# Three more row places in the adapted-attention layers, the output bias as its own step, retention's last transpositions among its gate projections, and the last pool sums on TensorE

## The chip, the cores and the metric

The kernel runs on the 8 cores of one Trainium2 chip. Each core computes one sequence of the batch by itself; the cores do not talk to each other. The metric is the device time of one launch in microseconds (us), taken on the slowest core. Five engines of a core run their own instruction queues: PE (TensorE, matrix products), DVE (VectorE), ACT (ScalarE), POOL (GpSimd) and SP, which here only starts transfers (DMA). They wait for each other by semaphores.

## The reference, cut to what matters

One sequence has 2048 tokens of width 1024. Four layers follow each other, each with a residual sum and a layer norm without weights ahead of it:

```
x = x + attn_a(layernorm(x))     # causal softmax attention, 16 heads of 64, projections q, k, v, o
x = x + ffn(layernorm(x))        # full attention, its q, k, v, o weights adapted (below), biases on each
x = x + attn_b(layernorm(x))     # retention: v is scanned along the tokens, y = q*state, layer norm of y,
                                 # times silu(x @ Wg.T), then @ Wo.T
x = x + ffn(layernorm(x))        # the same as the second, with the same weights
```

The adapted weights of `ffn` come from a gate: the mean of the layer's normed input over all tokens, two small products, the best 2 of 8 experts, and for each of q, k, v, o a low-rank product that is added to the main weight. So nothing of `ffn` can be projected until every token tile of the layer before has been normed and summed.

## The kernel before, in words

The program names the layers `a`, `f1`, `b`, `f2`. A token tile is 128 tokens; there are 16, numbered `t` or `tt` from 0. The residual rows live in memory (tensor `Xs`, at the start `xin`, at the end `y`); on the core there is only their normed and transposed form, in the arenas `XA` and `XB`. A layer reads its input from one arena (`ARENA[L][0]`) and keeps its attention output (`ctx`) in the other.

**What happens to a token tile at the end of a layer.** Two output projections `O` of 8 matmuls each (128x512, line 992) make the halves of the tile. DVE adds each to the tile's residual row in place (line 1266). The row was loaded (`xl`, line 1586) into one of three row places, number `t % 3`. In the layers `f1` and `f2` POOL has before that added the output bias `OB` to the whole row (line 1534, called `ob` here); before the change this add is part of the step `xl`, so it stands in POOL's queue where the load stands in SP's. After the second half the row is stored (`xs`, line 1591) and, but for `f2`, normed: statistics on DVE (`ln1`, lines 1337 and 1340), the reciprocal root on POOL (`rs`, lines 1442 and 1445), the norm itself on DVE (`ln2`, line 1349), which reads a 128x1024 row of f32 and writes bf16. PE transposes the normed tile (`T`, line 996), DVE or ACT copies it to the next layer's arena (lines 1272 and 1147). In `a` and `b`, POOL also adds the normed tile to a running sum (`pr`, line 1454), which the gate of the next layer reads. Then the next row is loaded into the place, tile `t + 3`: SP waits until the store of tile `t` has landed and `ln2` of it has run.

**What sets the order.** A planner (`Plan`, `build_plan`) writes one list of steps; each engine's part of the program walks this list and takes what is its own. So each queue holds its steps in the list's order, and a step that waits holds up everything behind it on its engine. The steps `rs` and `ln2` are put 1 and 2 groups of PE work behind the tile's last projection (`norm`).

**Where the tiles are done.** In `a`, `f1` and `f2` the projections of tiles 0 to 7 lie in the attention of the second half of the tokens (`second_half`), where ACT's exponentials run nearly without a gap. Tiles 8 to 15 come after it, alone (`tail`, `o_dense`). I call this stretch the tail of the layer. It starts when the attention of the last head pair has been divided by its sums: DVE takes reciprocals (line 1309), copies them apart in 8 copies (line 1316) and multiplies (line 1326); PE has by then done 7 of 8 matmuls of the first four projections. In `b` the tokens go in 4 chunks of 512 (`c`). A chunk projects v and q for 8 slices (`bv`, `bq`, line 1000), then sums over the slices on PE (`bs`, line 1005), then projects the gate for 8 slices (`bg`). DVE and POOL norm the slices (`bz`), ACT applies scale and silu, and DVE multiplies (`bap`, line 1380). The output projections of the 4 tiles of the chunk before lie among the v and q projections; tiles 12 to 15 form the tail of `b`. Their `T` of the last two tiles of a chunk stand right ahead of `bs`.

**The gate** (lines 1094 to 1105): after the tail of `a` or `b`, PE sums the running sum over the partitions by 8 f32 matmuls of one column (line 1094). It waits for the last `pr` and for all evictions.

Of the kernel before, what the change touches and what calls it, by code (L numbers as in the profile page):

```python
# [13 lines left out]
T = 2048  # L14
# [8 lines left out]
FFN = ("f1", "f2")  # L23

# [30 lines left out]
class Plan:  # L55
# [38 lines left out]
    def special(self, a):  # L94
        if a[0] == "rs":
            self.count("rs", ("rs",) + a[1:])
        elif a[0] == "ln2":
            self.count("ln2", ("ln2",) + a[1:])
        self.step(*a)
        if a[0] == "ln2":  # L100
            L, t = a[1:]
            if L in ("a", "b"):
                self.count("pr", ("pr", L, t))
                self.step("pr", L, t)
            if t + 3 < NT:
                self.xl(L, t + 3)
# [33 lines left out]
    def after(self, grp):  # L140
# [11 lines left out]
        elif k == "O" and a[1] == 1:  # L152
            t = a[0]
            self.step("xs", L, t)
            if L != "f2":
                self.norm(L, t)
            elif t + 3 < NT:
                self.xl(L, t + 3)
# [40 lines left out]
def build_plan():  # L199
    P = Plan()  # L200

    def o_items(L, tiles, by="v"):
# [252 lines left out]
    def second_half(L, k_ch):  # L455
# [4 lines left out]
        if L == "a":  # L460
            out.insert(at_[NP - 2], ("f_pre", "f1"))
# [120 lines left out]
    def b_layer():  # L582
# [8 lines left out]
        for c in range(4):  # L591

            o = {}
            if c >= 1:
                its = o_items("b", list(range(4 * c - 4, 4 * c)))
                n_o = [i for i, g in enumerate(its) if isinstance(g, Grp) and g.kind == "O" and g.args[1] == 0]
                o = {3: its[:n_o[1]], 4: its[n_o[1]:n_o[2]], 6: its[n_o[2]:n_o[3]], 7: its[n_o[3]:]}
# [12 lines left out]
            for d in range(ND):  # L610
# [54 lines left out]
def build_program():  # L665
# [147 lines left out]
    dXL = [sem(f"d_xl{i}") for i in range(3)]  # L813
    dXS = [sem(f"d_xs{i}") for i in range(3)]
# [21 lines left out]
    n = {"xl": [0] * 3, "xs": [0] * 3}  # L836
    for st in P.steps:
        if st[0] == "xl":
            s_ = st[2] % 3
            n["xl"][s_] += 16  # L840
            dv[("xl", st[1], st[2])] = n["xl"][s_]
        elif st[0] == "xs":
            s_ = st[2] % 3
# [45 lines left out]
    with nc.Block("main") as blk:  # L889
# [3 lines left out]
        def _(t_):  # L893
# [113 lines left out]
            for st in P.steps:  # L1007
# [75 lines left out]
                elif st[0] == "gate":  # L1083
# [104 lines left out]
        def _(v_):  # L1188
# [15 lines left out]
            for st in P.steps:  # L1204
                if st[0] == "att_on":
                    v.wait_ge(dCO, NCO)
                if st[0] == "fe" and st[1].by == "v":
# [52 lines left out]
                    elif k == "O":  # L1260
# [3 lines left out]
                        v.wait_ge(dXL[tt % 3], dv[("xl", L, tt)])  # L1264
# [39 lines left out]
                elif st[0] == "gn":  # L1304
# [14 lines left out]
                    else:  # L1319
                        cl = i - 8  # L1320
                        v.wait_ge(vSF, gn_at[5 + 2 * cl])
                        if g.L in FFN and g.h == 0 and g.p == 0:

                            for tt in (13, 14, 15):
                                v.wait_ge(dXS[tt % 3], dv[("xs", "a" if g.L == "f1" else "b", tt)])
# [3 lines left out]
                elif st[0] == "ln1":  # L1329
                    _, L, tt = st  # L1330
                    if L == "x":
                        v.wait_ge(dXL[tt % 3], dv[("xl", L, tt)])
# [98 lines left out]
        def _(g_):  # L1431
# [5 lines left out]
            for st in P.steps:  # L1437
# [128 lines left out]
        def _(p_):  # L1566
            p = Eng(p_)
            for st in P.steps:
                if st[0] == "xl":
# [4 lines left out]
                    else:  # L1574
# [4 lines left out]
                        if tt >= 3:  # L1579
                            p.wait_ge(dXS[tt % 3], dv[("xs", L, tt - 3)])  # L1580
                            if L != "f2":
                                p.wait_ge(vXN, at[("ln2", L, tt - 3)])
                        if L != "a":
                            before = {"f1": "a", "b": "f1", "f2": "b"}[L]
                            p.wait_ge(dXS[tt % 3], dv[("xs", before, tt)])
                    p_.dma_start(xo(L, tt), dr[SRC[L]][tt * 128:(tt + 1) * 128, :]
                                 ).then_inc(dXL[tt % 3], 16)
                elif st[0] == "xs":
# [3 lines left out]
                                 ).then_inc(dXS[tt % 3], 16)  # L1592
# [33 lines left out]
            for i in range(3):  # L1626
# [57 lines left out]
```

## Time and profile before

| | us |
|---|---|
| median of the three runs shown | 2783.66 |
| lowest and highest of them | 2586.55, 2851.24 |
| the profiled execution | 2594.22 |
| its longest core (5), first to last instruction | 2592.5 |
| its shortest core (1) | 2567.9 |

On core 5 PE is busy for 85% of the span, ACT for 58%, DVE for 51% and POOL for 24%. The profile was taken of one execution; all rows below are of its core 5, and all times in them count from the core's first instruction.

### The profile page before, as it was taken

Reading aid. Unit: us, or ns where it says so; the run is one execution under the profiler, and the core shown is the slowest. Engines: PE = TensorE matmul, PEld = TensorE weight load, DVE = VectorE, ACT = ScalarE, POOL = GpSimd, SP = SyncE. Lnnn points to the kernel's source line nnn. Section 1 sums busy time; section 2 is a strip of 40 time slices with the busy share of each in tenths; the row PEclk is TensorE's granted clock in tenths of the full one; section 3 lists DMA queues with packets and bytes.
Section 4 is the critical chain, followed back from the end, with each engine's and each line's share of the span. In section 5 each row is a group of like instructions: output and inputs, shape, how many; then the busy total and the mean of one; then the engine's idle time right before and its main releaser. Section 6 shows DMA issues by size and latency. Waiting matters only on the chain.

```text
span 2592.5 us, 39690 instructions; the slowest of 8 cores (2567.9 to 2592.5 us)
## 1 busy us (share of the span) xinstructions
PE 2201.5 (85%) x13480; PEld 766.5 (30%) x13480; DVE 1317.0 (51%) x2018; ACT 1498.3 (58%) x1494; POOL 635.0 (24%) x762
## 2 busy tenths in 40 slices
PE   4888799998699989879899599996989989788886
PEld 2322222223342222222222244443422222222222
DVE  4367635656453444434554567775445454433443
ACT  1234377773007777879999032221057777899991
POOL 4244333434111111112212323333021211021112
PEclk9989899999699999999999899997999999999998
DMA  8111322224400000012211531135200000021003
GB/s 173 25 25 25 62 46 65 66 74 129 148 9 24 25 26 25 17 49 58 58 42 50 130 73 66 65 114 154 74 25 26 25 25 17 17 74 33 33 33 122
DMA packets 49570, 151.10 MB, mean 58 GB/s; under 512 B 6624, under 2 KB 8800, under 8 KB 49120
## 3 DMA queue, kind: packets, MB, share of 16 engines
q1 hardware_dynamic: 33984, 124.80, 14.8%
q0 software_dynamic: 13376, 23.07, 6.1%
q8 instruction: 115, 1.88, 0.3%
q10 hardware_dynamic: 2016, 0.70, 0.1%
q14 instruction: 79, 0.65, 0.1%
HBM read 138.06 MB, written 33.55 MB: 66 GB/s over the span
## 4 chain that ended last, share of the span: by engine, by line
PE 59%; ACT 12%; DVE 12%; issue 8%; DMA 5%; POOL 3%; ACTq 0%; DVEq 0%; POOLq 0%; SPq 0%
ACT MISC L1135 11%; PE psd L1045 10%; PE psx L1064 8%; PE psx L974 6%; PE psx L970 6%; PE psx L1079 6%; PE psx L992 4%; PE psd L965 3%; PE psx L1000 3%; PE psx L965 3%; PE psd L1000 3%; PE psx L978 1%; DVE MISC L1316 1%; DMA XB<-Xs 1%; DVE MISC L1309 1%
## 5 line engine op out<-in xcount | busy, mean ns | idle before, releaser
L1135 ACT ACTIVATE MISC<-psd,NEGC 128x1024 bf16<-128x1024 f32 (+3 forms) x1344 | 1389.0, 1083 | 659.8 <-PE psd L1047 644.0
L1045 PE MATMUL psd<-MISC,KT 64*128 64x512 bf16 (+3 forms) x1344 | 510.2, 382 | 96.5 <-ACT MISC L1135 88.7
L1047 PE MATMUL psd<-MISC,KT 64*128 64x512 bf16 (+3 forms) x1344 | 514.8, 385 | 0.0
L1064 PE MATMUL psx<-MISC,VT 128*64 128x512 bf16 (+3 forms) x1344 | 424.1, 391 | 19.2 <-POOL MISC L1528 7.4
L1066 PE MATMUL psx<-MISC,VT 128*64 128x512 bf16 (+3 forms) x1344 | 425.9, 392 | 0.0
L1045 PEld LDWEIGHTS psd<-MISC,KT 64*128 64x128 bf16 x1344 | 124.4, 93 | 610.7 <-issue 603.5
L1521 POOL TENSOR_TENSOR MISC<-KT 128x512 bf16<-128x512 bf16 x96 | 108.3, 1128 | 565.8 <-DVE KT L1223 507.8
L1316 DVE COPY MISC<-MISC 32x512 f32<-32x512 f32 x384 | 218.6, 569 | 9.1
L1079 PE MATMUL psx<-MISC,ONESs 128*32 128x512 bf16 (+3 forms) x2688 | 218.9, 388 | 0.0
L1521 POOL TENSOR_TENSOR MISC<-MISC 128x512 bf16<-128x512 bf16 x96 | 106.8, 1113 | 339.2 <-DVE MISC L1230 282.4
L1309 DVE RECIPROCAL MISC<-MISC 128x128 f32<-128x128 f32 x192 | 170.0, 922 | 4.6
L1064 PEld LDWEIGHTS psx<-MISC,VT 128*64 128x64 bf16 x1344 | 97.9, 108 | 199.1 <-issue 198.1
L1534 POOL TENSOR_TENSOR XB<-XB,MISC 128x1024 f32<-128x1024 f32 x32 | 75.3, 2359 | 271.0 <-DMA XB<-Xs 271.0
L974 PE MATMUL psx<-XB,MISC 128*128 128x512 bf16 x504 | 128.9, 388 | 12.9 <-DVE MISC L1230 8.8
L1230 DVE TENSOR_SCALAR MISC<-psx,CST 128x512 bf16<-128x512 f32 x63 | 46.6, 739 | 163.3 <-PE psx L974 163.3
L1528 POOL TENSOR_TENSOR MISC<-MISC,TRIs 128x256 bf16<-128x256 bf16 x128 | 86.4, 676 | 159.3 <-ACT MISC L1135 157.6
L1047 PEld LDWEIGHTS psd<-MISC,KT 64*128 64x128 bf16 x1344 | 124.5, 93 | 0.0
L1223 DVE TENSOR_SCALAR KT<-psx,CST 128x512 bf16<-128x512 f32 x58 | 43.5, 751 | 158.6 <-PE psx L970 158.6
L970 PE MATMUL psx<-XB,MISC 128*128 128x512 bf16 x464 | 123.1, 394 | 0.0
L1066 PEld LDWEIGHTS psx<-MISC,VT 128*64 128x64 bf16 x1344 | 97.9, 108 | 0.0
L1301 DVE COPY MISC<-psx 128x512 f32<-128x512 f32 x48 | 33.2, 691 | 125.3 <-PE psx L1079 124.7
L1266 DVE TENSOR_TENSOR XB<-psx,XB 128x512 f32<-128x512 f32 x45 | 30.6, 682 | 130.2 <-PE psx L992 109.1
(187 smaller groups left out, 2707.6 us busy)
## 6 DMA issues: line engine op xcount, KB each, us to landing
XB<-Xs SPq DMA_DIRECT2D x40, 512.0 KB, 4.1
MISC<-fWq SPq DMA_DIRECT2D x32, 512.0 KB, 3.5
Xs<-XA SPq DMA_DIRECT2D x24, 512.0 KB, 3.0
Xs<-XB SPq DMA_DIRECT2D x24, 512.0 KB, 3.0
XB<-xin SPq DMA_DIRECT2D x16, 512.0 KB, 6.3
XA<-xin SPq DMA_DIRECT2D x16, 512.0 KB, 5.1
MISC<-fWk SPq DMA_DIRECT2D x16, 512.0 KB, 3.6
y<-XB SPq DMA_DIRECT2D x16, 512.0 KB, 3.0
```

Source lines behind the costliest of these rows:

```text
L965: return mm(o, xt(L, i, m * 128, 128), W1[:, i * 1024 + j * 512:i * 1024 + (j + 1) * 512], start=st, stop=sp)
L970: return mm(o, w[:, i * 128:(i + 1) * 128], xt(L, i, ch * CH, CH), start=st, stop=sp)
L974: return mm(o, w[:, i * 128:(i + 1) * 128], xt(L, i, h * 1024 + cl * CH, CH), start=st, stop=sp)
L1045: mm(pd[:, s:CH], ks[0:64, :], q[0:64, cl * CH + s:(cl + 1) * CH], start=True, stop=True, tile_position=(0, 0))
L1047: mm(pd[:, CH + s:2 * CH], ks[64:128, :], q[64:128, cl * CH + s:(cl + 1) * CH], start=True, stop=True, tile_position=(64, 0)).then_inc(sSC, 1)
L1064: mm(PVB[cl][0:64, s:CH], va[:, 0:64], r[:, s:CH], start=(c.tk == 0), stop=lastk, tile_position=(0, 0))
L1066: ins = mm(PVB[cl][64:128, s:CH], va[:, 64:128], r[:, CH + s:2 * CH], start=(c.tk == 0), stop=lastk, tile_position=(0, 64))
L1079: ins = mm(DENB[q0:q0 + 32, s:CH], ONES[:, 0:32], r[:, hd * CH + s:(hd + 1) * CH], start=(c.tk == 0), stop=lastk, tile_position=(0, q0))
L1135: s_.activation(r, pd, AF.Exp, bias=NEGC[:, col:col + 1], scale=sc).then_inc(aEX, 1)
L1309: chain(v_.reciprocal(d, d))
L1316: ins = v_.tensor_copy(RB[cl][32 * q:32 * q + 32, :], DN[q0:q0 + 32, :])
L1521: g_.tensor_mul(SQ[:, o:o + CH], src, src).then_inc(gSQ, 1)
```

## The change

- `slot` and `follower`: in `f1` and `f2`, tiles 11, 12 and 13 get row places of their own (3 to 5), in the second half of the input arena, which is free once the last q is projected. Their loads (`xl`) stand in the list ahead of the projections of tile 6, in the second half's attention. Tile `t` up to 7 is followed in its place by `t + 3`; tiles 8 and 9 by 14 and 15.
- The bias add is a step `ob` of its own. It stands where the projections of the tile before it begin.
- In `b`, the transpositions of the last two tiles of a chunk stand behind the gate projections of slices 1 and 3 and are copied by ACT instead of DVE. Tile 11 is projected in the tail instead of chunk 3.
- The running sum on POOL stops after 14 tiles. The gate's sum over the partitions adds the last two tiles from their normed rows: 16 bf16 matmuls of one column more.

```diff
+def slot(L, t):
+    return t % 3 + 3 if L in FFN and 11 <= t <= 13 else t % 3
+
+def follower(L, t):
+    if L not in FFN:
+        return t + 3
+    return t + 3 if t <= 7 else t + 6
...
-            if L in ("a", "b"):
+            if L in ("a", "b") and t < NT - 2:
                 self.count("pr", ("pr", L, t))
                 self.step("pr", L, t)
-            if t + 3 < NT:
-                self.xl(L, t + 3)
+            self.load_next(L, t)
...
             self.begin(grp)
+            if grp.kind == "O" and grp.args[1] == 0:
+                self.ob(grp.L, grp.args[0] + 1)
...
     def xl(self, L, t):
-        if L in FFN:
+        self.step("xl", L, t)
+
+    def ob(self, L, t):
+
+        if L in FFN and t < NT:
             self.count("ob", ("ob", L, t))
-        self.step("xl", L, t)
+            self.step("ob", L, t)
+
+    def load_next(self, L, t):
+
+        n = follower(L, t)
+        if n < NT and slot(L, n) == slot(L, t):
+            self.xl(L, n)
...
-                out += [("xl", L, x) for x in range(3)]
+                out += [("xl", L, x) for x in range(3)] + [("ob", L, 0)]
...
-        if L == "a":
-            out.insert(at_[NP - 2], ("f_pre", "f1"))
+
+        out[at_[NP - 2]:at_[NP - 2]] = [("f_pre", "f1")] if L == "a" else [("xl", L, t) for t in (11, 12, 13)]
...
-            o = {}
+            o, late = {}, []
             if c >= 1:
-                its = o_items("b", list(range(4 * c - 4, 4 * c)))
+
+                its = o_items("b", list(range(4 * c - 4, 4 * c - c // 3)))
                 n_o = [i for i, g in enumerate(its) if isinstance(g, Grp) and g.kind == "O" and g.args[1] == 0]
-                o = {3: its[:n_o[1]], 4: its[n_o[1]:n_o[2]], 6: its[n_o[2]:n_o[3]], 7: its[n_o[3]:]}
+                o = {3: its[:n_o[1]], 4: its[n_o[1]:n_o[2]], 6: its[n_o[2]:-2]}
+                if c < 3:
+                    o.update({6: its[n_o[2]:n_o[3]], 7: its[n_o[3]:-2]})
+                late = [Grp("T", "b", g.args, ND, 0.35, "a") for g in its[-2:]]
...
                 if d >= 2:
                     bap(c, d - 2)
+                if d % 2 and late:
+                    P.dense([late.pop(0)])
...
     def b_tail():
-        o_dense("b", list(range(12, NT)))
+        o_dense("b", list(range(11, NT)))
...
     def xo(L, t):
         a, base = scratch(L, t)
+        if slot(L, t) >= 3:
+            base += 8192
         base += (t % 3) * 2048
...
-                    t.wait_ge(gPR, at[("pr", src, NT - 1)])
+                    t.wait_ge(gPR, at[("pr", src, NT - 3)])
+                    t.wait_ge(vXN, at[("ln2", src, NT - 1)])
                     for dt in range(ND):
-                        ins = mm(BK[4][:, 16 + dt:17 + dt], ACC[src][:, dt * 128:(dt + 1) * 128], ONESF[:],
-                                 start=True, stop=True)
+                        o = BK[4][:, 16 + dt:17 + dt]
+                        mm(o, ACC[src][:, dt * 128:(dt + 1) * 128], ONESF[:], start=True, stop=False)
+                        mm(o, xn(src, NT - 2)[:, dt * 128:(dt + 1) * 128], ONES[:, 0:1],
+                           start=False, stop=False)
+                        ins = mm(o, xn(src, NT - 1)[:, dt * 128:(dt + 1) * 128], ONES[:, 0:1],
+                                 start=False, stop=True)
...
-                elif st[0] == "xl" and st[1] in FFN:
+                elif st[0] == "ob":
                     _, L, tt = st
                     g.wait_ge(dCO, NCO)
-                    g.wait_ge(dXL[tt % 3], dv[("xl", L, tt)])
+                    g.wait_ge(dXL[slot(L, tt)], dv[("xl", L, tt)])
                     g_.tensor_add(xo(L, tt), xo(L, tt), OB).then_inc(gOB, 1)
...
-                        if tt >= 3:
-                            p.wait_ge(dXS[tt % 3], dv[("xs", L, tt - 3)])
-                            if L != "f2":
-                                p.wait_ge(vXN, at[("ln2", L, tt - 3)])
+                        for t0 in range(NT):
+                            if follower(L, t0) == tt and slot(L, t0) == slot(L, tt):
+
+                                p.wait_ge(dXS[slot(L, t0)], dv[("xs", L, t0)])
+                                if L != "f2":
+                                    p.wait_ge(vXN, at[("ln2", L, t0)])
+                        if slot(L, tt) >= 3:
+                            p.wait_ge(sFL, at[("f", "Q", L, 1, NP - 1, 1)])
```

The order that comes out of it, at two places. In both, a name says what is written, then what is read; the line numbers of the changed kernel are other ones for the same steps.

First POOL, from the last attention of `f1` into its tail. L1534 (before) and L1573 (changed) are `ob`, L1442 and L1445 (L1481 and L1484) are `rs`. Before:

```order
L1561 DMA VT<-bWg 128x1024 x8
L1442 TENSOR_SCALAR RSD0<-MV0 128x1
L1445 TENSOR_TENSOR RSD0<-RSD0,PWR 128x1
L1534 TENSOR_TENSOR XB<-XB,MISC 128x1024
L1442 TENSOR_SCALAR RSD1<-MV1 128x1
L1445 TENSOR_TENSOR RSD1<-RSD1,PWR 128x1
L1534 TENSOR_TENSOR XB<-XB,MISC 128x1024
```

Changed:

```order
L1600 DMA VT<-bWg 128x1024 x8
L1573 TENSOR_TENSOR XB<-XB,MISC 128x1024 x2
L1481 TENSOR_SCALAR RSD0<-MV0 128x1
L1484 TENSOR_TENSOR RSD0<-RSD0,PWR 128x1
L1481 TENSOR_SCALAR RSD1<-MV1 128x1
L1484 TENSOR_TENSOR RSD1<-RSD1,PWR 128x1
L1573 TENSOR_TENSOR XB<-XB,MISC 128x1024
L1481 TENSOR_SCALAR RSD0<-MV0 128x1
L1484 TENSOR_TENSOR RSD0<-RSD0,PWR 128x1
L1573 TENSOR_TENSOR XB<-XB,MISC 128x1024
```

The adds of tiles 9 and 10 now stand ahead of the tail's first `rs`, and those of 11 to 15 each right behind an `rs`. Before, each stood behind an `rs` too, but was the add of a row that had just been asked for.

Second PE, in `b`, at the end of chunk 1's v and q projections (L1000 or L1034 with `KT`). L992 or L1026 is `O`, L996 or L1030 `T`, L1005 or L1039 `bs`, L1000 or L1034 with `VT` the gate projection. Before:

```order
L992 MATMUL psd1<-W1,XB 128x512 x8
L996 MATMUL psd1<-IDENTBs,XB 128x128 x8
L996 MATMUL psx0<-IDENTBs,XB 128x128 x8
L1005 MATMUL psx1<-MISC,ONESs 128x512 x8
L1005 MATMUL psx2<-MISC,ONESs 128x512 x8
L1000 MATMUL psx3<-XA,VT 128x512 x8
L1000 MATMUL psd0<-XA,VT 128x512 x16
```

Changed:

```order
L1026 MATMUL psd1<-W1,XB 128x512 x8
L1039 MATMUL psd1<-MISC,ONESs 128x512 x8
L1039 MATMUL psx0<-MISC,ONESs 128x512 x8
L1034 MATMUL psx1<-XA,VT 128x512 x8
L1034 MATMUL psx2<-XA,VT 128x512 x8
L1030 MATMUL psx3<-IDENTBs,XB 128x128 x8
L1034 MATMUL psd0<-XA,VT 128x512 x16
L1030 MATMUL psd1<-IDENTBs,XB 128x128 x8
```

The two `T` moved from ahead of `bs` to behind the second and the fourth gate projection; chunks 2 and 3 have the same.

## Rows read from the trace of the kernel before

**Rows 1.** One line of the cores: span and mean granted TensorE clock (1 is full speed).
```profile
core 5: 2592.5 us, clock 0.944
```

**Rows 2.** The page's chain that ended last, shares of the span by engine.
```profile
PE 59%; ACT 12%; DVE 12%; issue 8%; DMA 5%; POOL 3%; ACTq 0%; DVEq 0%; POOLq 0%; SPq 0%
```

**Rows 3.** Timeline, f1's tail: an ln2 while POOL is free.
```profile
1440.94 0.81 DVE L1349 TENSOR_SCALAR XB<-XB,MV,RSD 128x1024 bf16<-128x1024 f32 x1 [0.49 <-POOL RSD L1445]
```

**Rows 4.** Timeline, f1's tail: start us, us, engine line [idle before <-releaser]; PE, POOL.
```profile
1441.90 0.61 PE L996 MATMUL psx<-IDENTBs,XB 128*128 128x128 bf16 x8 [1.62 <-DVE XB L1349]
...
1450.90 2.34 POOL L1534 TENSOR_TENSOR XB<-XB,MISC 128x1024 f32<-128x1024 f32 x1 [10.07 <-DMA XB<-Xs]
...
1498.27 1.01 PE L996 MATMUL psd<-IDENTBs,XB 128*128 128x128 bf16 x8 [3.71 <-DVE XB L1349]
```

**Rows 5.** Timeline, a's tail: PE's transpositions of two tiles in a row.
```profile
634.66 0.61 PE L996 MATMUL psd<-IDENTBs,XA 128*128 128x128 bf16 x8 [0.32 <-DVE XA L1349]
...
639.04 0.61 PE L996 MATMUL psd<-IDENTBs,XA 128*128 128x128 bf16 x8 [0.33 <-DVE XA L1349]
```

**Rows 6.** Timeline near 53 us: POOL's rs, its next step, DVE's ln2.
```profile
52.99 0.57 POOL L1445 TENSOR_TENSOR RSD<-RSD,PWR 128x1 f32<-128x1 f32 x1
53.52 1.04 POOL L1521 TENSOR_TENSOR MISC<-MISC 128x512 bf16<-128x512 bf16 x1
...
53.66 1.45 DVE L1349 TENSOR_SCALAR XB<-XB,MV,RSD 128x1024 bf16<-128x1024 f32 x1 [1.31 <-POOL RSD L1445]
```

**Rows 7.** Timeline, f1's attention: DVE's eight copies and an ob.
```profile
1326.06 5.55 DVE L1316 COPY MISC<-MISC 32x512 f32<-32x512 f32 x8
...
1328.77 2.56 POOL L1534 TENSOR_TENSOR XB<-XB,MISC 128x1024 f32<-128x1024 f32 x1 [5.21 <-DMA XB<-Xs]
```

**Rows 8.** Timeline, the start of f1's tail.
```profile
1426.60 4.24 POOL L1561 DMA_DIRECT2D VT<-bWg  x8
...
1430.94 3.50 DVE L1316 COPY MISC<-MISC 32x512 f32<-32x512 f32 x8
```

**Rows 9.** Timeline, f2's tail.
```profile
2541.49 2.36 POOL L1534 TENSOR_TENSOR XB<-XB,MISC 128x1024 f32<-128x1024 f32 x1 [15.97 <-DMA XB<-Xs]
...
2546.80 3.50 DVE L1316 COPY MISC<-MISC 32x512 f32<-32x512 f32 x8
...
2557.77 7.07 PE L992 MATMUL psd<-W,XA 128*128 128x512 bf16 x32
...
2587.40 0.68 DVE L1266 TENSOR_TENSOR XB<-psx,XB 128x512 f32<-128x512 f32 x1
```

**Rows 10.** Timeline, b: PE around the ends of chunks 1 and 2.
```profile
1594.90 1.01 PE L996 MATMUL psx<-IDENTBs,XB 128*128 128x128 bf16 x8 [4.29 <-DVE XB L1349]
...
1601.11 1.89 PE L1000 MATMUL psx<-XA,VT 128*128 128x512 bf16 x8
...
1662.16 1.01 PE L996 MATMUL psd<-IDENTBs,XB 128*128 128x128 bf16 x8 [4.29 <-DVE XB L1349]
...
1668.87 5.34 PE L1000 MATMUL psx<-XA,VT 128*128 128x512 bf16 x24
```

**Rows 11.** Timeline, b: end of chunk 3 and the tail.
```profile
1722.39 0.68 DVE L1290 TENSOR_TENSOR MISC<-psd,MISC 128x512 bf16<-128x512 f32 x1
...
1735.46 0.69 DVE L1294 TENSOR_SCALAR MISC<-psd 128x512 f32<-128x512 f32 x1 [1.03 <-PE psd L1005]
...
1766.44 0.69 DVE L1266 TENSOR_TENSOR XA<-psd,XA 128x512 f32<-128x512 f32 x1 [7.11 <-PE psd L992]
```

**Rows 12.** Timeline, b's end: the last T, pr, copy, and the gate's first matmuls.
```profile
1784.84 1.01 PE L996 MATMUL psx<-IDENTBs,XA 128*128 128x128 bf16 x8 [3.44 <-DVE XA L1349]
1784.90 2.12 POOL L1454 TENSOR_TENSOR MISC<-MISC,XA 128x1024 f32<-128x1024 f32 x1 [1.19 <-DVE XA L1349]
1785.94 1.01 ACT L1147 COPY XB<-psx 128x1024 bf16<-128x1024 bf16 x1 [3.44 <-PE psx L996]
1787.31 3.55 PE L1094 MATMUL psx<-ONESF,MISC 128*128 128x1 f32 x16 [1.46 <-POOL MISC L1454]
```

More of the change, by code:

```diff
@@ L156, in after @@
                 self.norm(L, t)
-            elif t + 3 < NT:
-                self.xl(L, t + 3)
+            else:
+                self.load_next(L, t)
         elif k == "EV" and a[1] == 1:
@@ L255, in do @@
             P.xl(st[1], st[2])
+        elif st[0] == "ob":
+            P.ob(st[1], st[2])
         elif st[0] == "wl":
@@ L812, in build_program @@
     gMK, gSQ, gOB = sem("g_mask"), sem("g_sq"), sem("g_ob")
-    dXL = [sem(f"d_xl{i}") for i in range(3)]
-    dXS = [sem(f"d_xs{i}") for i in range(3)]
+    dXL = [sem(f"d_xl{i}") for i in range(6)]
+    dXS = [sem(f"d_xs{i}") for i in range(6)]
     dRW = [sem(f"d_raw{i}") for i in range(11)]
@@ L835, in build_program @@
     dv = {}
-    n = {"xl": [0] * 3, "xs": [0] * 3}
+    n = {"xl": [0] * 6, "xs": [0] * 6}
     for st in P.steps:
         if st[0] == "xl":
-            s_ = st[2] % 3
+            s_ = slot(st[1], st[2])
             n["xl"][s_] += 16
@@ L842, in build_program @@
         elif st[0] == "xs":
-            s_ = st[2] % 3
+            s_ = slot(st[1], st[2])
             n["xs"][s_] += 16
@@ L1324, in _ @@
                             for tt in (13, 14, 15):
-                                v.wait_ge(dXS[tt % 3], dv[("xs", "a" if g.L == "f1" else "b", tt)])
+                                v.wait_ge(dXS[slot("b", tt)], dv[("xs", "a" if g.L == "f1" else "b", tt)])
                         ins = v_.tensor_mul(ctx(g.L, g.p, g.h * 1024 + cl * CH, CH), PVF[cl], RB[cl])
@@ L1371, in _ @@
                     if c == 0 and d == 0:
-                        for tt in (13, 14, 15):
-                            v.wait_ge(dXS[tt % 3], dv[("xs", "f1", tt)])
+                        for tt in range(10, NT):
+                            v.wait_ge(dXS[slot("f1", tt)], dv[("xs", "f1", tt)])
                     elif c == 2 and d == 0:
                         for tt in (5, 6, 7):
-                            v.wait_ge(dXS[tt % 3], dv[("xs", "b", tt)])
+                            v.wait_ge(dXS[slot("b", tt)], dv[("xs", "b", tt)])
                         v.wait_ge(gPR, at[("pr", "b", 7)])
@@ L1578, in _ @@
                             p.wait_ge(sFL, at[("base", L)])
-                        if tt >= 3:
-                            p.wait_ge(dXS[tt % 3], dv[("xs", L, tt - 3)])
-                            if L != "f2":
-                                p.wait_ge(vXN, at[("ln2", L, tt - 3)])
+                        for t0 in range(NT):
[5 more added lines that the diff above has]
+                            p.wait_ge(sFL, at[("f", "Q", L, 1, NP - 1, 1)])
+                        if L == "b" and tt < 3:
+                            for t0 in (11, 12, 13):
+                                p.wait_ge(dXS[slot("f1", t0)], dv[("xs", "f1", t0)])
+                                p.wait_ge(vXN, at[("ln2", "f1", t0)])
                         if L != "a":
                             before = {"f1": "a", "b": "f1", "f2": "b"}[L]
-                            p.wait_ge(dXS[tt % 3], dv[("xs", before, tt)])
+                            p.wait_ge(dXS[slot(before, tt)], dv[("xs", before, tt)])
                     p_.dma_start(xo(L, tt), dr[SRC[L]][tt * 128:(tt + 1) * 128, :]
-                                 ).then_inc(dXL[tt % 3], 16)
+                                 ).then_inc(dXL[slot(L, tt)], 16)
                 elif st[0] == "xs":
@@ L1625, in _ @@
                     p_.dma_start(rawplace(L, s_), src).then_inc(dRW[s_], 16)
-            for i in range(3):
+            for i in range(6):
                 p.wait_ge(dXS[i], xs_end[i])
```

9 lines of the change are left out of this document (5 added, 4 removed).

## The prediction, made before the changed kernel was run

> **What bounds the kernel now.** I read the cores first: the longest has a mean granted clock of 0.944 [rows 1], so TensorE works at its full level nearly everywhere. Then the chain of waits: PE holds 59% of it, ACT and DVE 12% each, POOL 3% [rows 2]. In the attention PE and ACT keep each other busy and this change leaves them alone. Then the waits of each engine and, for the stretches in which PE waits, the timeline: the tails of `f1` and `f2`, the ends of the chunks of `b`, and the gate.
>
> In `f1`'s tail the transposition of tile 8 starts at 1441.90 and that of tile 15 at 1498.27 [rows 4]: 8.05 us a tile. The tail of `a` has the same projections and norms without bias, and where its loads are in time PE transposes every 4.38 us (634.66, 639.04) [rows 5]. The difference is the chain through one row place: store, load of 4 us, bias add of 2.34 us for which POOL had waited 10.07 us [rows 4].
>
> **f1's tail.** The change takes the loads of tiles 11 to 13 out of this chain and gives those of 14 and 15 six tiles of time. If nothing else held the norms, the tail would take 7 x 4.38 = 30.7 instead of 56.4 us: 25.7 saved. But the bias adds now start the moment POOL reaches them, and something of DVE needs them gone. At 53 us POOL ends the power of an `rs` (52.99) and begins its next step at 53.52; DVE's `ln2`, released by that power, is entered at 53.66 and takes 1.45 us [rows 6] where it takes 0.81 with POOL free [rows 3]: it ends at 55.11, 0.55 after POOL's step of 1.04 us. So `ln2` stood still while POOL worked. In the changed queue exactly such a pair, `rs` and then an `ob`, stands at tiles 9 to 13. With a bias add of 2.34 us, begun 0.04 before the power's end X, `ln2` ends at X + 2.30 + 0.55 = 2.85 instead of X + 0.1 + 0.81 = 0.91: 1.94 us lost, 5 times, 9.7 us. The bounds are 0, if `ln2` comes first, and 2.34 each.
>
> The adds of tiles 9 and 10 now stand behind the weight transfers that POOL issues until 1430.84, and DVE's eight copies start at 1430.94 [rows 8]. In `f1`'s attention eight such copies took 5.55 us with one bias add in their middle, against 3.50 without [rows 7, 8]: 2.05 more, and there the add itself took 2.56. Two adds cost between 4.1 and 4.7, and all of it lies on the path, since PE waits for the copies' result; I take 4.6. Last, PE has now 2 us without work in each tile and will do some of its matmuls at 1.2 GHz; I take 1 us (0 to 9, see the rivals). Saved: 25.7 - 9.7 - 4.6 - 1.0 = **10.4 us**.
>
> **f2's tail.** No norms here. PE does 32 matmuls in 7.07 us, 0.216 each, until 2564.84 [rows 9]; by then 52 of the tail's 100 are done, counted in the timeline. From there rows come late. With all rows there the last 48 end at 2575.2, the last eviction at 2576.1 instead of 2588.1 [rows 9]: 12.0 saved, the last store behind it being the same. POOL's queue has here tiles 10, 11, 12 and 13 in a row; tile 10's add starts when its load lands, at 2541.49, so those of 12 and 13 run from 2546.2 to 2550.9, over the copies that start at 2546.80 [rows 9]. By the price above: 1.75 for the rest of the first, 2.34 for the second, 4.1. With stores and loads of 3 to 6 us as before, tile 14's load lands near 2566 and tile 15's near 2572, each ahead of its eviction. Saved: **7.9 us**.
>
> **b, chunks 1 and 2.** PE idles 4.29 us until the last `T` starts at 1594.90, and the gate projections start at 1601.11 [rows 10]: 10.50 us, in which only the 16 matmuls of `bs` (3.45 at 0.216) are left; they now come without a stop ahead, so at the full clock. The `T` costs 0.45 later. 6.6 saved. Chunk 2 in the same way: 4.29 before 1662.16, gate at 1668.87, so 11.0 - 3.45 - 0.45 = 7.1. What hides DVE's work there is the lead of PE over DVE, 8 banks. DVE gets `ln2` between the two `bs` evictions and POOL's `pr` of 2.12 us then lies over the next products of two arrays, so the chain behind `bs` starts 2 us later against PE than before; I take 0.5 us for each chunk (0 to 2.5). Saved: **12.7 us**. The two `T` copies on ACT are hidden: ACT waits for DVE at every second slice.
>
> **b, chunk 3 and tail.** `bs` now follows the projection of slice 7 and waits for DVE's product, which ends at 1723.07; `bs` then ends at 1726.7 and its second eviction starts at 1726.95 instead of 1735.46 [rows 11]. The chain of `bz` and `bap` that bounds this stretch moves by 8.5. Tile 11's projections fill PE's wait for it, but add one tile at 4.39 us to a tail whose first eviction comes at 1754.6 instead of 1766.44 [rows 11]. The first `T` comes 5.2 behind that, as before, then four tiles: the last `T` at 1777.4 instead of 1784.84 [rows 12], 7.4 less. The loads of tiles 14 and 15 now both hang on stores inside the tail, among the weight loads; 1 us for that. Saved: **6.4 us**.
>
> **The gate, twice.** The sum waited for `pr`, which ended at 1787.02; the copy of the last `T` by ACT, for which it waits too, ended at 1786.95 [rows 12]. So dropping two `pr` brings 0.07 us. The 16 added matmuls have no row. Eight bf16 transpositions, each a weight load and few columns, take 1.01 us at the lower clock, 0.126 each; the f32 passes beside them take 0.222 [rows 12]. So 1.0 (at the full clock) to 3.6, and by the nearest row 2.0: **3.7 us lost** for both gates.
>
> The Trainium skill ("TensorE: Matmul & The Clock Gate", section "LDWEIGHTS (loading the stationary operand)") prices a weight load by its columns, 1.2 of them in a nanosecond, whatever the type; as an estimate from that page the 16 cost 1.7 us, and the sum would be 0.5 us better.
>
> **Sum.** 10.4 + 7.9 + 12.7 + 6.4 - 3.7 = 33.7 us, 1.3% of the profiled execution: 2594.2 - 33.7 = **2560 us**. The second half's loads and bias adds are costed at nothing: ACT's exponentials cover them, and the first tile's add stands as before. The profiled execution stands with the lowest of the three runs; their median, 2783.66, is 7.3% above it. The same saving from the median would give 2750, and nothing in the trace says which kind of run the changed kernel will show.
>
> **Rivals.**
>
> A. POOL does not hold up DVE, or loses the race: then the 9.7, 4.6 and 4.1 come back, 2560 - 18.4 = 2542. For it: evictions with one PSUM input are not slowed by a bias add in any row. Against: rows 6 and 7, where `ln2` and the copies are. The Trainium skill ("SBUF — State Buffer", section "SBUF: two separate sides") says that the two share a port pair that whichever starts first keeps for its whole instruction; by that rule A would need `ln2` to start first, and the trace agrees [rows 6]. 17%.
>
> B. The clock and the lead fail. Bursts of 16 matmuls with 2 us pauses fall to 1.2 GHz in `f1`'s tail: 6.9 + 1.0 us a tile instead of 6.3, 9 us more; and DVE uses up its lead in `b`, 2 us more in each chunk. 2560 + 13 = 2573. For it: two transpositions behind waits of 3.4 to 4.3 us took 1.01 instead of 0.61 [rows 10, 12]. Against: behind 1.6 us it took 0.61 [rows 4]. 18%.
>
> C. Slower: PE, now denser, is granted less clock over the whole run. Price: 59% of the span is PE on the chain, 1530 us; a mean clock of 0.944 x (1 - d) adds 1530 x d. It decides from d = 2.2% (0.923), and is over 2% slower from 5.6% (0.891). At 0.90, 2560 + 71 = 2631. Against: the clock falls here only after PE has idled. 4%.
>
> D. The change does not do what it says for the last tiles: SP's queue holds store 9 behind load 14, so 15 still comes late in `f1` and `f2`, 4 us in each: 2568. Against: six tiles of time are over 25 us. 6%.
>
> The forecast has 55%.
>
> **Range and chances.** Of its own the forecast reaches from 2545 to 2575 by the bounds above (gate 2 better or 3.3 worse, norms half hit or wholly, chunks). A takes the low end to 2538. The high end has to hold the other kind of run too, which two of three shown were: 2783.66 - 34, with some spread, 2785. A measurement of this kernel can tell about 2% from no change, 51.9 us. Beyond it lie half of A, a few of the forecast's own cases, and runs that fall apart between the two kernels: 23% faster. Slower by over 2% is half of C and such runs: 4%. Within 2%: 73%.
>
> **What the changed profile would show.** Right: `T` in `f1`'s tail every 6.3 us from the second on, `ln2` at 2.7 us or more beside an `ob`, the last `T` some 45 us behind the first; copies of 7 to 8 us instead of 3.50 in both adapted tails; no wait of PE before `bs` in chunks 1 and 2; the gate's first group at 5 to 6 us instead of 3.55; no wait of POOL for a landing in the tails. Wrong: `T` at 4.4 us steps (A), steps of 8 us with matmuls of 0.43 (B), a clock under 0.93 with PE never idle (C), POOL waiting for the load of tile 15 (D).

## The result, and the profile after

The changed kernel took 2555.68 us (median of four, 2553.22 to 2559.19); the kernel before, with one more run, 2685.11 (2583.66 to 2851.24). In two of the four executions of the kernel before the cores of a die were granted a lower clock; the comparison leaves such executions out, here and below, and gives a ratio of **0.9887 (95%: 0.9863 to 0.9911)**: 1.1% faster, 29 us of 2585, the mean of the other two (2583.66 and 2586.55). The profiled execution of the changed kernel took 2555.45, forecast 2560. The profiled execution of before, 2594.22, from which the sum was made, was itself 9 us above those two, so the saving, forecast at 33.7, is the better measure.

The lines of the cores and the chain, where [rows 1, 2] stood:

```profile
core 1: 2553.9 us, clock 0.952
```

```profile
PE 59%; DVE 13%; ACT 12%; issue 9%; DMA 3%; POOL 2%; ACTq 0%; DVEq 0%; SPq 0%; POOLq 0%
```

The same markers (first reciprocal of a tail, transpositions, first `bs` and first v projection of a chunk, start of the last eviction) can be read on all 8 cores of both traces. A chunk is counted from its first v projection to that of the next. Means over the cores, in us:

| stretch | before | changed | saved | forecast |
|---|---|---|---|---|
| f1's tail, reciprocal to last `T` | 70.35 | 58.73 | 11.6 | 10.4 |
| b, chunk 1 (its v and q, `bs`, gate) | 66.73 | 64.36 | 2.4 | 6.1 |
| b, chunk 2 | 67.54 | 64.84 | 2.7 | 6.6 |
| b, chunk 3 and tail, to last `T` | 102.21 | 95.87 | 6.3 | 6.4 |
| both gates, last `T` to the sum's end | 12.17 | 13.10 | -0.9 | -3.7 |
| f2's tail, reciprocal to last eviction | 44.05 | 36.63 | 7.4 | 7.9 |
| sum | | | 29.5 | 33.7 |

The 29.5 agree with the ratio. What these stretches leave (attention above all, 2213 us) became 6.0 us shorter. In the ten other kernels below, whose attention is the changed kernel's, it lies between 2.8 shorter and 3.5 longer. So I take the 6.0 for scatter, though they lie outside of what the ten show, and claim nothing of them.

f1's tail of the changed kernel, core 1, timeline (start us, us, engine line [idle before <-releaser]); the answers to [rows 3, 4, 8]:

```profile
1427.79 4.73 POOL L1573 TENSOR_TENSOR XB<-XB,MISC 128x1024 f32<-128x1024 f32 x2
1428.05 7.84 DVE L1355 COPY MISC<-MISC 32x512 f32<-32x512 f32 x8
...
1443.35 0.61 PE L1030 MATMUL psx<-IDENTBs,XB 128*128 128x128 bf16 x8 [1.13 <-DVE XB L1388]
...
1446.57 2.34 POOL L1573 TENSOR_TENSOR XB<-XB,MISC 128x1024 f32<-128x1024 f32 x1
1446.71 2.75 DVE L1388 TENSOR_SCALAR XB<-XB,MV,RSD 128x1024 bf16<-128x1024 f32 x1 [0.48 <-POOL RSD L1484]
1449.61 0.61 PE L1030 MATMUL psd<-IDENTBs,XB 128*128 128x128 bf16 x8 [2.20 <-DVE XB L1388]
...
1483.28 1.01 PE L1030 MATMUL psd<-IDENTBs,XB 128*128 128x128 bf16 x8 [3.31 <-DVE XB L1388]
```

POOL no longer waits for a landing. It starts the add 0.14 us ahead of `ln2`, and `ln2` takes 2.75 instead of 0.81 and ends 0.55 behind it. The transpositions come every 6.26 us five times, then twice every 4.32 (no add stands ahead of the last two `ln2`), and the eight copies take 7.84 instead of 3.50. f2's tail, core 1, against [rows 9]: four adds run in a row until 2521.82, and their last 5.5 us lie over the copies.

```profile
2512.21 9.61 POOL L1573 TENSOR_TENSOR XB<-XB,MISC 128x1024 f32<-128x1024 f32 x4 [17.18 <-DMA XB<-Xs]
2516.32 7.98 DVE L1355 COPY MISC<-MISC 32x512 f32<-32x512 f32 x8
...
2549.95 0.69 DVE L1305 TENSOR_TENSOR XB<-psx,XB 128x512 f32<-128x512 f32 x1 [0.90 <-PE psx L1026]
```

In b, core 1, chunk 1, against [rows 10]: `bs` begins at 1573.51 without a wait of PE ahead of it, but a new wait, of 2.49 us, stands ahead of the seventh gate projection. L1403 is DVE's first product behind `bs`, L1493 `pr`, L1191 a silu.

```profile
1577.45 0.81 DVE L1388 TENSOR_SCALAR XB<-XB,MV,RSD 128x1024 bf16<-128x1024 f32 x1 [0.69 <-POOL RSD L1484]
1578.47 2.12 POOL L1493 TENSOR_TENSOR MISC<-MISC,XB 128x1024 f32<-128x1024 f32 x1 [1.19 <-DVE XB L1388]
1578.97 2.17 DVE L1403 TENSOR_TENSOR MISC<-MISC 128x512 f32<-128x512 f32 x1
...
1590.13 0.60 ACT L1191 ACTIVATE VT<-psx 128x512 bf16<-128x512 f32 x1
1590.87 5.30 PE L1034 MATMUL psx<-XA,VT 128*128 128x512 bf16 x16 [2.49 <-ACT VT L1191]
```

The windows of that place (stretch, us, busy time of PE, PEld, DVE, ACT, POOL, then PEclk, DMA share, GB/s):

```profile
1573.50:1588.30 14.80, 14.80 (x81) 7.07 (x79) 10.29 (x13) 2.93 (x4) 5.41 (x6) 1.00 0.22 86
1588.30:1590.87 2.57, 0.08 (x1) 0.03 (x1) 2.47 (x2) 2.54 (x4) 2.43 (x3) 1.00 0.00 0
1590.87:1593.40 2.53, 2.53 (x9) 1.02 (x10) 2.53 (x4) 2.53 (x4) 1.41 (x1) 0.69 0.00 0
1593.40:1596.00 2.60, 2.60 (x9) 0.97 (x8) 2.50 (x4) 2.60 (x6) 2.28 (x2) 0.64 0.00 0
```

Behind the wait the granted clock is 0.69 and 0.64, between its two levels (1.2 and 2.4 GHz, 0.5 and 1 here), and the 16 matmuls take 5.14 us (to 1596.01) instead of 3.45. The stretch from the first gate projection to the next chunk's v grew from 13.81 to 19.05 us: 2.49 for the wait, 1.69 for the slower matmuls and 0.9 for the two transpositions are 5.1 of these 5.2. Last b's tail and the gate, against [rows 11, 12]:

```profile
1732.40 1.29 DVE L1305 TENSOR_TENSOR XA<-psd,XA 128x512 f32<-128x512 f32 x2 [3.42 <-PE psd L1026]
...
1750.78 0.69 DVE L1305 TENSOR_TENSOR XA<-psd,XA 128x512 f32<-128x512 f32 x1 [2.05 <-DMA XA<-Xs]
...
1756.73 1.01 PE L1030 MATMUL psx<-IDENTBs,XA 128*128 128x128 bf16 x8 [3.38 <-DVE XA L1388]
...
1759.36 0.56 PE L1130 MATMUL psx<-ONESF,MISC 128*128 128x1 f32 x2 [1.62 <-ACT XB L1186]
1759.78 0.17 PE L1131 MATMUL psx<-ONESs,XA 128*128 128x1 bf16 x1
1759.81 0.17 PE L1133 MATMUL psx<-ONESs,XA 128*128 128x1 bf16 x1
1759.84 0.57 PE L1130 MATMUL psx<-ONESF,MISC 128*128 128x1 f32 x2
```

A group of one f32 and two bf16 columns comes every 0.48 us; in the kernel before an f32 column came every 0.43. From the first matmul of the sum to the last one's end it is 3.97 us instead of 3.54, and to PE's next step 4.39 instead of 3.96: 0.43 more.

### The profile page after: what moved, and what is told of

Same layout as the page of the kernel before. It is cut to its first block, busy times and chain, and to the rows that moved or that the text cites. A ratio compares the mean times of both kernels' runs of the same rounds, so it can differ in the third digit from the quotient of the medians.

```text
span 2553.9 us, 39739 instructions; the slowest of 8 cores (2536.5 to 2553.9 us)
## 1 busy us (share of the span) xinstructions
PE 2187.3 (86%) x13512; PEld 764.5 (30%) x13512; DVE 1336.4 (52%) x2011; ACT 1504.3 (59%) x1501; POOL 626.4 (25%) x758
## 3 DMA queue, kind: packets, MB, share of 16 engines
q1 hardware_dynamic: 33984, 124.80, 14.4%
## 4 chain that ended last, share of the span: by engine, by line
PE 59%; DVE 13%; ACT 12%; issue 9%; DMA 3%; POOL 2%; ACTq 0%; DVEq 0%; SPq 0%; POOLq 0%
ACT MISC L1174 11%; PE psd L1079 10%; PE psx L1098 8%; PE psx L1008 6%; PE psx L1004 6%; PE psx L1113 6%; PE psx L1026 4%; PE psd L999 3%; PE psx L999 3%; PE psx L1034 3%; PE psd L1034 2%; DVE MISC L1355 2%; PE psd L1026 2%; PE psx L1012 1%; DVE STT L1376 1%
## 5 line engine op out<-in xcount | busy, mean ns | idle before, releaser
L1026 PE MATMUL psx<-W,XA 128*128 128x512 bf16 x312 | 81.7, 388 | 22.0 <-DVE XA L1365 17.7
L1305 DVE TENSOR_TENSOR XB<-psx,XB 128x512 f32<-128x512 f32 x45 | 30.6, 682 | 125.3 <-PE psx L1026 107.5
```

What stands on the lines that cost most here:

```text
L1026: return mm(o, ctx(L, i, tt * 128, 128), W1[:, i * 1024 + j * 512:i * 1024 + (j + 1) * 512], start=st, stop=sp)
```

## The experiments

Each kernel is edited from the changed one. Stage lengths are means over the 8 cores of one profiled execution, and ratios are to the kernel before. Stretches whose code an edit leaves alone show the scatter: f2's tail 35.55 to 37.64, chunk 3 with the tail 95.87 to 96.69, and chunk 1 63.09 to 64.36, since the fall of the clock there came on some cores and not on others.

| kernel | f1's tail | chunk 1 | chunk 2 | chunk 3 + tail | gates | f2's tail | ratio (95%) |
|---|---|---|---|---|---|---|---|
| changed | 58.73 | 64.36 | 64.84 | 95.87 | 13.10 | 36.63 | 0.9887 (0.9863 to 0.9911) |
| e1_ob_waits | 45.05 | 63.93 | 64.83 | 96.20 | 13.11 | 32.15 | none |
| e2_t_last | 58.73 | 62.08 | 63.51 | 97.46 | 13.02 | 36.87 | 0.9883 (0.9862 to 0.9905) |
| e3_pr_waits | 58.73 | 64.53 | 61.79 | 96.09 | 13.10 | 37.64 | 0.9879 (0.9831 to 0.9926) |
| e4_ob_split | 53.62 | 63.09 | 64.83 | 96.69 | 13.14 | 37.70 | one run |
| e5_t11_chunk | 58.73 | 64.15 | 64.83 | 96.92 | 13.05 | 36.26 | 0.9885 (0.9870 to 0.9900) |
| e6_all_t_early | 45.06 | 61.61 | 61.67 | 96.03 | 13.11 | 32.01 | 0.9786 (0.9773 to 0.9799) |
| e7_all_t_last | 45.06 | 60.59 | 62.02 | 97.21 | 13.03 | 32.18 | 0.9792 (0.9779 to 0.9805) |
| e8_ffn_only | 58.74 | 66.55 | 67.49 | 102.49 | 12.16 | 35.57 | 0.9923 (0.9908 to 0.9938) |
| e9_ob_pr | 45.05 | 61.61 | 61.67 | 96.37 | 13.12 | 32.06 | 0.9799 (0.9737 to 0.9861) |
| e10_gate_old | 58.73 | 63.73 | 64.81 | 96.32 | 12.19 | 35.55 | one run |

**e1: the adds wait for DVE.** In both tails the adds of tiles 9 to 15 wait until DVE has divided the last head pair. In f1's tail the step `ob` of tile t + 2 also stands behind `ln2` of tile t in the list, and waits for it.

```diff
-            if grp.kind == "O" and grp.args[1] == 0:
+            if grp.kind == "O" and grp.args[1] == 0 and not (grp.L == "f1" and grp.args[0] >= 9):
                 self.ob(grp.L, grp.args[0] + 1)
...
+            if L == "f1" and t >= 8:
+                self.ob(L, t + 2)
...
                     g.wait_ge(dXL[slot(L, tt)], dv[("xl", L, tt)])
+                    if tt >= 9:
+                        g.wait_ge(vCX, at[("cx", L, 1, NP - 1)])
+                    if tt >= 10 and L == "f1":
+                        g.wait_ge(vXN, at[("ln2", L, tt - 2)])
```

> The changed kernel, but POOL's bias adds of tiles 9 to 15 wait until DVE has divided the last head pair, and in f1 that of tile t + 2 also waits until ln2 of tile t has ended. Nothing is left out. Theory 1 (an add that POOL has begun keeps DVE's SBUF-only instructions out until it ends; the same add laid beside evictions, statistics and matmuls costs nothing): ln2 in f1's tail 0.81 us instead of 2.75, transpositions every 4.4 us instead of 6.26, the eight copies 3.50 us instead of 7.84 in both tails; f1's tail shorter by 4.3 + 5 x 1.87 = 13.7 us, f2's by 4.3, the kernel near 2538 us. Rival 1 (the step of 6.26 us is the price of the add itself, wherever it lies: it slows evictions and statistics as it slowed ln2): steps stay over 6 us, the time stays at 2555. Rival 2 (with the adds gone from beside ln2, rs waits behind the add on POOL): steps of 4.4 + 0.5 to 2.3 us, the time between 2541 and 2550.

The four runs, 2558.87 to 2671.04, lie too far apart for a ratio, so no time of the whole kernel shows this edit alone (e6 and e9 below contain it); the stages of the profiled one, 2558.87, decide. Core 6, f1's tail (L1390 is `ln2`, L1378 the statistics, L1579 the add):

```profile
1456.44 2.36 POOL L1579 TENSOR_TENSOR XB<-XB,MISC 128x1024 f32<-128x1024 f32 x1 [1.06 <-DVE XB L1390]
1456.44 0.61 PE L1032 MATMUL psx<-IDENTBs,XB 128*128 128x128 bf16 x8 [0.71 <-DVE XB L1390]
...
1456.99 1.29 DVE L1378 BATCH_NORM_STATS2 STT<-XB 128x6 f32<-128x512 f32 x2
...
1459.81 0.81 DVE L1390 TENSOR_SCALAR XB<-XB,MV,RSD 128x1024 bf16<-128x1024 f32 x1
1460.77 0.61 PE L1032 MATMUL psd<-IDENTBs,XB 128*128 128x128 bf16 x8 [0.27 <-DVE XB L1390]
```

The same add of 2.36 us now lies beside the statistics, which take the 1.29 they always took, and costs nothing; `ln2` is back at 0.81, and the copies take 3.49. The seven steps between transpositions take 30.6 us, 4.38 each, and the first `T` comes 14.4 behind the reciprocal instead of 18.8. f1's tail is 13.7 us shorter, as worked out ahead, f2's 4.5. Rivals 1 and 2 fall.

**e4: the add in two halves.**

```diff
-                    g_.tensor_add(xo(L, tt), xo(L, tt), OB).then_inc(gOB, 1)
+                    x = xo(L, tt)
+                    g_.tensor_add(x[:, 0:512], x[:, 0:512], OB[:, 0:512])
+                    g_.tensor_add(x[:, 512:1024], x[:, 512:1024], OB[:, 512:1024]).then_inc(gOB, 1)
```

> The changed kernel, but each bias add is two instructions on POOL, of 512 columns each instead of one of 1024. Theory 1 (the two engines take turns on the port instruction by instruction): ln2 behind an add in f1's tail gets in between the halves: 0.8 + about 1.2 minus the lead = 1.6 us instead of 2.75, and the second half then waits for ln2; transpositions every 5.1 us instead of 6.26. The eight copies cost the same 7.8, since POOL's halves fill in between, or less if copies take turns with halves. Rival (both share the port's bandwidth, or DVE waits until POOL's queue is empty): ln2 stays at 2.7 us and the step at 6.26.

One run, 2564.64 us, its slowest core at a granted clock of 0.945; the stages decide here too. Core 5:

```profile
1459.83 1.26 POOL L1574 TENSOR_TENSOR XB<-XB,MISC 128x512 f32<-128x512 f32 x1
1459.97 1.67 DVE L1388 TENSOR_SCALAR XB<-XB,MV,RSD 128x1024 bf16<-128x1024 f32 x1 [0.49 <-POOL RSD L1484]
1461.05 1.72 POOL L1575 TENSOR_TENSOR XB<-XB,MISC 128x512 f32<-128x512 f32 x1
```

`ln2` gets in between the halves (1.67 us), the second half then stands for it (1.72), and the step is 5.18 us. They take turns, instruction by instruction; they do not share. The eight copies gain nothing, 8.13 us on that core. So f1's tail is 5.1 us shorter by the split, against 13.7 by the waits.

**e2: both late transpositions behind the last gate projection,** that is behind the loop over the slices.

```diff
-                if d % 2 and late:
-                    P.dense([late.pop(0)])
+            P.dense(late)
```

> The changed kernel, but in b both late transpositions of a chunk stand behind its last gate projection instead of behind the second and fourth. Theory 1 (the two transpositions take two of PE's 8 result banks, so the seventh gate projection waits for ACT's first silu, which hangs on DVE's chain behind bs): PE runs all 8 gate projections without a wait, and v of the next chunk starts as soon as the third silu has freed its bank, about 20.5 us behind bs instead of 22.5 (19.2 before the change); 2.0 us less in each of chunks 1 and 2, the kernel near 2551 us. Rival (DVE's chain from bs to the next bs bounds the chunk whatever PE does): v starts earlier, but PE then waits for DVE in the v and q projections, the distance from one bs to the next stays at 64.8 us, the time at 2555. Second rival (ACT's transposed copies now come behind all silus and hold up squares of the next chunk): longer by 1 to 2 us a chunk, 2558.

v now starts 19.8 us behind `bs` instead of 22.1 and 22.5, a little sooner than the 20.5 expected, but from v to the next `bs` it is 43.7 instead of 42.3, since PE waits there for silus (0.28 and 0.84 us). Chunks 1 and 2 are 2.3 and 1.3 shorter, chunk 3 with the tail 1.6 longer: 2.0 in sum, half of what theory 1 gave, and no difference in time. The wait ahead of the seventh projection is gone, so the banks were what it hung on. The other half is what the rival said: PE waits for the same releases further on.

**e3: the running sum of a chunk's last tile waits.**

```diff
                     g.wait_ge(vXN, at[("ln2", L, tt)])
+                    if L == "b" and tt in (3, 7, 10):
+                        g.wait_ge(vBS, 2 * (tt // 4 + 1 if tt < 8 else 3) + 1)
```

> The changed kernel, but in b POOL's running sum of the last tile of a chunk (tiles 3, 7, 10) waits for DVE's variance of bs, so that it runs while DVE waits for ACT's logarithm and exponential. Theory 1 (the chain bs, DVE's products, ACT, first silu sets when PE gets a bank, and 1.49 us of it are DVE's first product standing still behind POOL's sum): the product takes 0.69 instead of 2.17 us, the first silu starts 1.5 us sooner behind bs (15.1 instead of 16.6), PE's wait ahead of the seventh gate projection is 1.0 instead of 2.5 us; each of chunks 1 to 3 shorter by 1.5 us or, if PE then also keeps its full clock, up to 3; the kernel near 2550 us. Rival (PE's own work or the clock sets it): the product is shorter, v of the next chunk starts as before, 2555 us.

Core 0, chunk 1:

```profile
1570.48 0.69 DVE L1403 TENSOR_TENSOR MISC<-MISC 128x512 f32<-128x512 f32 x1
...
1580.90 3.61 PE L1034 MATMUL psx<-XA,VT 128*128 128x512 bf16 x15 [1.00 <-ACT VT L1191]
```

The product takes 0.69 instead of 2.17, PE waits 1.00 instead of 2.49, and the matmuls behind it keep the full rate (3.61 us for a group that took 5.30; 15 of its 16 matmuls are in the trace). Chunk 2 is 3.05 us shorter: 1.5 of wait and 1.6 of clock. (In chunk 1, `bs` of cores 4 and 5 took 4.20 us instead of 3.45 in this execution, and their gate projections were slower too; e6 and e9, with the same wait, have 2.7 less there than the changed kernel.) Nothing moves in chunk 3, where the sum of tile 10 is over before DVE's product. The ratio does not tell e3 from the changed kernel, so these 3 us a chunk rest on the stages, and on e6 and e9.

**e5: tile 11 back in chunk 3.**

```diff
-                its = o_items("b", list(range(4 * c - 4, 4 * c - c // 3)))
+                its = o_items("b", list(range(4 * c - 4, 4 * c)))
...
-        o_dense("b", list(range(11, NT)))
+        o_dense("b", list(range(12, NT)))
```

> The changed kernel, but tile 11 is projected in chunk 3 of b again, with its transposition behind the fourth gate projection; the tail has tiles 12 to 15. Nothing is left out. Theory 1 (what the tail's start hangs on is DVE's chain behind bs, which the late transpositions alone bring forward; tile 11 in chunk 3 costs PE 3.5 us, of which 1.94 fill its wait for DVE, and takes 4.4 to 6 us out of the tail): bs of chunk 3 stands 42.3 us behind v instead of 40.5, from there to the tail's first eviction 31.0 as now, the tail 18.4 us instead of 24.3; 4 us less, near 2551. Rival (my step of the forecast: tile 11 in the tail is what fills PE's wait for the chain, so without it the chain or bs comes later): the tail's start moves back by 4 to 5 us, and the sum is 0 to 1 us worse, 2556.

My theory fell and the rival, the forecast's own step, held: `bs` of chunk 3 comes 1.8 later behind v, from there to the tail's first eviction it is 36.0 instead of 31.0, the tail 18.6 instead of 24.3; 1.0 us worse in sum, and 0.2 to 1.0 by the scatter of this stretch. The matmuls of tile 11 need nothing of chunk 3, so PE does 14 of them while DVE works on the last slices; those of tiles 12 to 15 must wait. And `pr` of tile 11 holds up the product (2.17 us) as in the other chunks.

**e6, e7 and e9: together.** e6 is e1, e3 (tiles 3, 7, 11) and e5; e7 adds e2; e9 is e1 and e3 alone.

> Three edits on the changed kernel: the bias adds wait as in e1, the running sum of tiles 3, 7 and 11 waits as in e3, tile 11 is projected in chunk 3 as in e5. If the parts add up: 18.2 us for the adds (13.7 in f1's tail, 4.5 in f2's), 5.4 for the sums in chunks 1 and 2, and 0 to 1.5 more in chunk 3, 4 for tile 11: 28 us less than the changed kernel, near 2528 us. If they do not (DVE's work bounds b, and what one edit brings another takes back): the two in b together bring 5 instead of 9, near 2532.

> As e6, with the late transpositions behind the last gate projection as in e2. e2 moved the chunks by 0.9 and 1.3 us; with the first silu 1.5 us sooner the seventh gate projection waits 1.0 us, of which this takes the rest away: 0.5 to 1 us less in each chunk than e6, near 2527 us. If ACT's releases of the banks, not PE's order, set when v of the next chunk starts: no difference to e6 within 1 us.

> The waits of e1 and e3 alone on the changed kernel; tile 11 stays in b's tail and the transpositions where the change put them. After e5 (tile 11 in the tail fills PE's wait for DVE's chain, and is worth 1 us) the theory says: f1's tail 45.1 us, f2's 32.1, chunks 1 and 2 at 61.7 us each as in e6, chunk 3 with the tail 95.9 as in the changed kernel; 23.6 us less than the changed kernel, the same as e6 within 1.5 us (near 2533). Rival (tile 11 in chunk 3 was worth something once the sum of tile 11 waits): 2 us or more slower than e6 by the stages.

e6 took 2535.64 us (median of six, lowest 2530.88), e7 2534.92, e9 2548.15 (lowest 2533.23; its interval is wide). The stages: e6 and e9 agree within 0.5 us, 24.0 and 23.7 below the changed kernel where e9 was to give 23.6. Tile 11's place is worth nothing that these runs can show, and of e6's 28 us the 4 for it did not come. e7's v starts 1 us earlier and its `bs` 1.4 later: the second expectation, that ACT's releases set the pace, fits (PE waits 0.28 and 0.84 us for silus there). By the ratios all three beat the changed kernel by 0.9 to 1.0%; e6 is 2.1% faster than the kernel before.

**e8: the part on f1 and f2 alone** (b and the gate as before).

> The part of the change on the adapted layers alone: row places of tiles 11 to 13 and the bias add as its own step; b and the gate as before. By the stages of the two traces this part is f1's tail (11.7 us) and f2's tail (7.5 us), with 0.7 behind f1's: 19 to 20 us less than the kernel before, near 2566 us beside 2585. If the parts lean on each other (loads of b's first rows, POOL's queue): b's chunks differ from those of the kernel before by over 1 us.

2569.50 us, ratio 0.9923: 20 us. f1's tail 58.74, f2's 35.57, b's stretches within 0.3 us of the kernel before. So this part alone gives the two tails that the changed kernel has, f2's within its scatter, and takes nothing from b; the other part was not run alone.

**e10: the gate as before.**

> The changed kernel with the gate of before: the running sum takes all 16 tiles, the sum over the partitions is 8 f32 matmuls. By the two traces the 16 matmuls of one column cost 0.38 us (3.92 instead of 3.54) for each gate and the dropped sums of tiles 14 and 15 bring nothing: the matmuls start 2.6 us behind the last transposition either way, and the gate group takes 3.54 us again. Rival (the dropped sum is worth its 2.13 us somewhere, since POOL's rs of tile 15 no longer stands behind it): a's tail or b's longer by up to 2 us with the old gate.

2557.71 us, one run. The gate groups take 3.54 us again, both gates 12.19 against 13.10, and a's tail is not longer (47.6 instead of 47.9 us), b's within its scatter. The dropped sums bring nothing, as forecast, and the 16 matmuls cost 0.43 us. (The 3.92 and 0.38 of the expectation end with the last f32 matmul and leave out the two bf16 ones behind it.)

## Why the prediction was right and where it was wrong

**f1's tail: right.** Forecast: loads off the chain 25.7, less 9.7 for `ln2`, 4.6 for the copies, 1.0 for the clock. The copies' price was 4.3, five steps of 6.26 against 4.38 make 9.4, and both went away together in e1, which shows that the adds' position was all of it. The 1.0 for the clock was not paid: some matmuls did run at the lower level (8 in 3.19 us at 1462.93, against 1.89), but the path runs through `ln2` and does not wait for them, so the clock half of rival B did not come either. (The sign "the last `T` some 45 us behind the first" did not follow from this sum, which gives 30.7 + 9.7 + 1.0 = 41.4; it was 39.9.) The Trainium skill ("SBUF — State Buffer", section "SBUF: two separate sides") calls the port pair that GpSimd shares with VectorE an exclusive lock: whichever starts first, a GpSimd instruction or a VectorE one in a two-port mode or with two SBUF inputs, keeps it for its whole instruction. The trace agrees: 2.75 us behind a whole add, 1.67 behind half of one, 0.81 when the add waits. So rival A, which needed DVE to win the race, did not come.

**f2's tail: right** (7.4 for 7.9), by the same price: with the adds behind the copies (e1) the tail is 11.9 us shorter than before, forecast 12.0, and the copies' price was 4.5 instead of 4.1.

**b, chunks 1 and 2: wrong, 5.1 us instead of 12.7, and this is the step that failed:** "What hides DVE's work there is the lead of PE over DVE, 8 banks ... I take 0.5 us for each chunk (0 to 2.5)." The lead was used up before anything could be hidden. A bank holds a group's result until DVE or ACT has copied it out; the two transpositions take two of the 8, so PE reaches the end of its banks two groups earlier, and the first release, by the first silu, comes 16.6 us behind the start of `bs`. Before it came at 15.1 to 16.8, although `bs` itself then took 4.4 to 6.0 us instead of 3.45: the chain did not shrink with it. I had counted `pr` over the product (it costs 1.5), but neither that the wait it feeds is not hidden at all nor that slower matmuls follow that wait. 2.5 of wait and 1.7 of slower matmuls, less the 0.5 set aside, are 3.7, about what was missing (3.7 and 3.9). e3 gives back 3 us a chunk, and with e2's order too (e7) chunks 1 and 2 save 6.1 and 5.5 against the kernel before: the forecast 6.1 and 6.6 are reached for the one, nearly for the other, once both are mended, though e7's chunk 3 and tail give back 1.3 of it. Rival B had this for 2 us a chunk; it was 3.8.

**b, chunk 3 and tail: right** (6.3 for 6.4), filler and all, by e5. The loads inside the tail cost 1.5 us (five tiles in 24.33 where 18.40 + 4.39 would be 22.8) instead of 1.

**The gate: the size was wrong,** 0.9 instead of 3.7 for both (and 2.0 a gate less the 0.07 for `pr` would have been 3.9). The nearest row, transpositions at 0.126, was too dear; the 16 matmuls cost 0.027 each, and why so little no run here shows. By the Trainium skill ("TensorE: Matmul & The Clock Gate", section "LDWEIGHTS (loading the stationary operand)") they were, as an estimate from its price of a weight load, 1.7 us a gate, four times what the trace shows.

**The sum.** Errors of both signs partly cancelled, which is luck: -7.6 in the chunks, +2.8 at the gates, +1.2 in f1's tail, -0.6 elsewhere, 33.7 - 4.2 = 29.5. That the changed kernel's time then came out below the forecast, 2555 for 2560, and not above it, is the starting point: the profiled execution of before was 9 us long. C and D did not happen: the clock is 0.952, and no eviction in the tails of f1 and f2 waits for a tile. (POOL does wait for the landings of 14 and 15 in f2's, 13.11 and 3.58 us on core 1, against my last list, but the adds end at 2537.28 and 2543.21 and their first evictions begin at 2544.90 and 2548.36.)

## What to carry to other kernels

When work on GpSimd is freed from a wait, ask what of VectorE it will now start just ahead of; a wait that puts it behind VectorE's SBUF-only instruction, beside evictions and statistics, can be worth more than the freed transfer (18 us here by the stages, for a few lines, against 20 for the new row places). A group moved into a stretch that runs ahead of its evictions costs a bank of lead, not only its own time: count banks to the first release. And a nearest row of another shape is a weak price: take it as an upper end, not as the value.

## What the runs showed of the hardware that I had not expected

- In chunk 1 of the changed kernel, the same wait of 2.49 us was followed by 16 matmuls in 5.14 us on six cores and in 3.45 us on two (cores 2 and 3); in chunk 2 on all eight by 5.1. After a wait of 1.00 us the clock held: the 16 took 3.45 us on all eight cores in chunk 2 of e3 and in both chunks of e6 and e9. Why two cores were spared is open.
- A bf16 matmul of one column between two f32 ones adds 0.027 us (0.43 / 16).
- One add of 2.36 us on POOL beside evictions (one PSUM input, 0.69 us) and `bn_stats` (1.29 us for two) on DVE slows neither.
